# Ten of sixteen probability blocks turned by DMA instead of eight, with six slots for halves and eight for turned blocks, in a masked attention kernel on one core

## The reference

```
h      = maximum(layernorm(x), 0)                 # (8192, 128), eps 1e-5
scores = einsum('nd,md->nm', h, ks)               # (8192, 8192)
scores = leaky_relu(scores, negative_slope=0.2)
scores = where(adj > 0, scores, -9e15)
attn   = softmax(scores, axis=1)
out    = x + einsum('nm,md->nd', attn, ks)
```

## Time and profile before

| | |
|---|---|
| median of 3 runs | 1658.87 us (1658.17 to 1659.25) |
| the profiled execution | 1658.6 us |
| its span in the profile | 1656.8 us |
| busy: TensorE, VectorE, ScalarE, GpSimd | 97%, 90%, 85%, 70% |
| HBM read, written | 276.82 MB, 4.19 MB |

### The profile page before, as it was taken

The page is one execution under the profiler, slowest core; times in us unless marked ns, Lnnn a source line. Parts: engine busy times, 40 slices in busy tenths (PEclk is TensorE's granted clock), DMA queues, the critical chain, the costliest instruction groups (busy, mean ns, idle before and its releaser), DMA issues.

```text
span 1656.8 us, 38135 instructions
## 1 busy us (share of the span) xinstructions
PE 1609.1 (97%) x13442; PEld 1181.7 (71%) x13442; DVE 1491.6 (90%) x2592; ACT 1400.4 (85%) x2081; POOL 1155.8 (70%) x1224
## 2 busy tenths in 40 slices
PE   5699999999999999999999999999999999999999
PEld 3477777777777777777777777777777777777777
DVE  7999899899899899999999999999998998998996
ACT  6688888888888888888888888888888888888887
POOL 1576776776776767767767767767767767767766
PEclk8999999999999999999999999999999999999999
DMA  7799999999999999999999999999999999999996
GB/s 235 196 230 261 253 264 256 248 265 269 249 263 254 254 262 263 253 261 255 254 265 259 253 260 253 264 266 248 262 260 256 263 262 248 268 258 244 272 253 127
DMA packets 641340, 417.78 MB, mean 252 GB/s; under 512 B 551040, under 2 KB 575616, under 8 KB 641152
## 3 DMA queue, kind: packets, MB, share of 16 engines
q1 hardware_dynamic: 641152, 415.34, 103.9%
HBM read 276.82 MB, written 4.19 MB: 170 GB/s over the span
## 4 chain that ended last, share of the span: by engine, by line
PE 70%; DVE 18%; issue 4%; ACT 2%; POOL 1%; DMA 0%; DVEq 0%; POOLq 0%
PE ps_out L386 20%; PE ps_T L371 10%; PE ps_out L387 10%; PE ps_scores L360 10%; PE ps_scores L362 10%; PE ps_scores L361 10%; DVE mask L573 8%; DVE scores L591 5%; DVE probsT_lo L600 2%; ACT probsT_hi L470 2%; DVE hT_hi L516 1%; DVE row_min L606 1%; DVE plain_max L609 1%; POOL keys_in L314 0%; PE ps_out L338 0%
## 5 line engine op out<-in xcount | busy, mean ns | idle before, releaser
L314 POOL TENSOR_TENSOR keys_in<-scores,keys_in 128x512 f16<-128x512 f32 x512 | 652.2, 1274 | 41.4
L591 DVE CUSTOM_DVE_ANT_0 scores<-ps_scores,mask,minus_scale 128x1024 f32<-128x1024 f32 x512 | 652.8, 1275 | 1.4 <-PE ps_scores L362 0.6
L312 POOL CAST keys_in<-scores 128x512 f16<-128x512 f32 x512 | 346.0, 676 | 402.3 <-ACT scores L462 402.0
L462 ACT ACTIVATE scores<-scores,neg_max 128x1024 f32<-128x1024 f32 x512 | 582.5, 1138 | 0.0
L453 ACT ACTIVATE scores<-scores 128x1024 f32<-128x1024 f32 x512 | 537.8, 1050 | 51.9 <-DVE pair_min L591 51.8
L600 DVE TENSOR_TENSOR probsT_lo<-ps_T,probsT_hi 128x512 f16<-128x512 f32 x512 | 350.2, 684 | 130.1 <-ACT probsT_hi L470 130.1
L470 ACT ACTIVATE probsT_hi<-ps_T 128x512 f16<-128x512 f32 x512 | 305.7, 597 | 186.1 <-PE ps_T L371 185.7
L386 PE MATMUL ps_out<-keys,probsT_hi 128*128 128x256 f16 x2048 | 392.8, 272 | 18.8 <-DVE probsT_lo L600 12.8
L360 PE MATMUL ps_scores<-keysT_hi,hT_hi 128*128 128x512 f16 x1024 | 391.2, 382 | 16.4 <-DVE keysT_lo L555 9.4
L361 PE MATMUL ps_scores<-keysT_lo,hT_hi 128*128 128x512 f16 x1024 | 390.5, 381 | 0.0
L362 PE MATMUL ps_scores<-keysT_hi,hT_lo 128*128 128x512 f16 x1024 | 390.1, 381 | 0.0
(11 more groups left out here) (52 smaller groups left out, 830.0 us busy)
## 6 DMA issues: line engine op xcount, KB each, us to landing
adj_in<-in_adj_dram SPq DMA_DIRECT2D x512, 512.0 KB, 5.1
keys_in<-keys_in SPq DMA_TRANSPOSE x512, 4.9
x_in<-in_x_dram SPq DMA_DIRECT2D x64, 64.0 KB, 2.1
keys_in<-in_L_gnn_ks_dram SPq DMA_DIRECT2D x8, 512.0 KB, 7.3
out_dram<-out_tile SPq DMA_DIRECT2D x64, 64.0 KB, 1.8
```

The costliest lines, as they stand in the source:

```text
L314: nc.gpsimd.tensor_tensor(half[:, BLOCK:2 * BLOCK], probs(t, b), half[:, 0:BLOCK], ALU.subtract) \
L462: nc.scalar.activation(s, s, ACT.Exp, bias=neg_max[:, t % 2:t % 2 + 1], scale=-SLOPE, accum_out=pair_sum[:, t % 2, p:p + 1]).then_inc(prob ...
L591: nc.vector.tensor_tensor_reduce(out=score_pair(q, p), in0=ps_scores[:, slots, :].rearrange("p s k -> p (s k)"), in1=mask[:, (p // 2) % 2, ...
```

## The change

`BY_DMA` takes blocks 4 and 12 as well. It then holds ten blocks, 1, 3, 4, 5, 7, 9, 11, 12, 13, 15, and `BY_PE` six, 0, 2, 6, 8, 10, 14. The slots for halves go from four to six and those for turned blocks from six to eight, fourteen of the sixteen that there is room for. All counts and waits follow from these tuples and sizes.

```
-    R_SLOTS = 4
+    R_SLOTS = 6
     X_SLOTS = 4
-    D_SLOTS = 6
+    D_SLOTS = 8
...
-    BY_DMA = tuple(b for b in range(BLOCKS) if b % 2 == 1)
+    BY_DMA = tuple(b for b in range(BLOCKS) if b % 2 == 1 or b in (4, 12))
     BY_PE = tuple(b for b in range(BLOCKS) if b not in BY_DMA)
```

## The result

The change made the kernel slower: 1699.34 us in the median of 4 runs (1697.12 to 1710.2) against 1658.71 for the kernel before (4 runs, 1658.17 to 1659.25), a ratio of 1.0258 [1.0228, 1.0288]. The forecast was 1622 and its range ended at 1698. What happened is the outcome of rival (b), a step of 25.6 us and 1700.

The account below looks back on a forecast made before the run. TensorE bounds the kernel before at 25.02 us a step, DMA afterwards at 24.35. 62 steps save 41.5 us, tail and start add 3.6 + 1: span 1619.9, time 1622, 8 in 10 range 1588 to 1698.

Parts of the forecast that it names:

- rival (b): DMA saturates under the mixed traffic; at a share of 1.16 a step takes 25.6 us, total 1700; chance 0.30.
- the mixed stretch: Fullest window mixing loads and transposes before the change, share 1.22 for 10 us; gave DMA's need of 24.35 us a step.
- The rival's own point of decision: DMA share in mixed traffic: below 29.7 / 25.02 = 1.19, the step is longer than before.
- The floor by 210 GB/s: DMA step from separate rates: eight loads at 1.38 us, ten transposes at 1.25, some 0.4 for x and store: 23.9 us.
- TensorE's need: TensorE's step without two blocks' transposes (0.88 us) and two short waits (0.49 us): 23.65 us instead of 25.02.
- both waits: TensorE's waits each step, 0.14 us for hT_lo and 0.35 us for block 12's probsT_lo, expected to go.
- rival (a): DMA keeps up and GpSimd or TensorE bounds, 23.65 to 24.0 us a step, total 1589; chance 0.20.
- GpSimd's need: GpSimd's step: ten split_half 18.0 us, normalise 1.7, four mask meetings at 1.03 each: 23.8 us.
- collisions with masks: GpSimd waiting while VectorE makes a mask, four times a step at 1.03 us each.
- some 8: Microseconds until GpSimd has block 7's half ready after getting pair 2's probabilities: 7.1, some 8 with a mask.
- Rival (c): Hidden dependency chain around a step's end holds the step at 24.9 to 25.0 us, total 1656 to 1664; chance 0.08.
- the ring: Chain around a step's end: TensorE, probsT_hi, split_h, add_mask, minimum and a mask stretched to 2.1 us; step near 25.0 us.

Follow-up runs that it names:

- the new order alone: Kernel before (eight blocks by DMA) with split_h ahead of split_probs_lo in slot 14 and slot 0's mask made at slot 14's end: 1627.19 us, 0.9811.
- the turns apart: Kernel after, with SP issuing the adj load between a slot's two turns instead of ahead of both: 1739.43 us, 1.0487.
- the fastest kernel: Kernel after with nine blocks by DMA (4 not turned), split_h ahead of split_probs_lo and slot 0's mask at slot 14's end: 1608.65 us, 0.9702.

## Why the prediction was wrong

**The step that failed** is the choice of the ceiling, "I take 24.35: the mixed stretch is the row nearest to the new mixture". The work of DMA was right: predicted 29.7 us of packets a step, measured 1.15 x 25.67 = 29.5. The divisor was not. It was taken as 1.22, from ten microseconds; over whole steps the share is 1.13 to 1.15 in the kernels with nine to eleven blocks, while short windows go far above it, to 1.35 in the kernel after. 29.7 / 1.15 = 25.8 would have been slower than before. The other end of the range, 1.16, gave rival (b) its 25.6. That this lies so near is in part luck: the 1.16 came from a stretch of loads alone, without a transpose. No row of the kernel before shows the new mixture at its limit, so the trace could bound the ceiling poorly and not fix it. The rival's own point of decision, a share of 1.19, was the right question. And with 0.30 on a rival at 1700, a range of 8 in 10 that ends at 1698 was too narrow by the prediction's own numbers.

That it is the load on DMA, and not something that came with it, is shown: without the two transfers' bytes 1699 us become 1612, with half the bytes of `adj` and every issue in its place 1618; without the work on their halves nothing changes, and the slots change nothing. Not shown is which limit of DMA it is. The engines' packets may be at their ceiling, or too few transfers may fit in the queue at a time, or a turned block simply comes too late for a step of this order: fewer bytes relieve all three. A longer distance between turn and use (`ADD_LAG`) would tell the last from the others; it was not tried.

The Trainium skill ("DMA: Bandwidth & Descriptors", section "Latency and other measured facts") gives 261 GB/s for transposing DMAs with a non-contiguous middle dimension. The slices full of transposes in the earlier trace rows show 203 to 223 but for one stretch of 255 to 278, which "210 GB/s wherever a slice was full of them" passes over. So the figure agrees with that one stretch and not with the others. The floor by 210 GB/s, 23.9 us, was still 1.8 us short of the measured step: rates taken from loads alone and from turns alone don't give the mixture's.

**TensorE's need** was put at 23.65 us. With DMA out of the way it is 24.2 (24.20 and 24.21 with the extra turns or half of `adj` gone). TensorE is busy for 1475.89 / 1500 x 24.20 = 23.81 of it; the rest is the wait for `probsT_lo`, which moved from block 12's copy in slot 2 to block 8's in slot 14. The prediction had both waits go and looked for no new one. The upper value, 24.14 "if both waits stay", was nearer, though for another wait. So rival (a), 1589, was out of reach in this order of instructions: with DMA relieved the chip gives 1612.

**GpSimd's need** was put at 23.8 us and is 1276.96 / 1500 x 25.67 = 21.9 of busy time. That leaves 21.9 - 19.7 = 2.2 us for collisions with masks, where 4.1 had been counted. A sixth of its work taken away changed nothing.

**Latency.** The halves were as early as worked out, 8.2 us for "some 8". Landing grew little, 5.3 us for 4.9. The 4.4 us for which the finished half of block 7 stood behind other issues at SP were missing from the sum, as was the 6.0 us landing of this turn, for 4.9 in the median.

**Rival (c)** did not happen with ten blocks, and its 0.08 was fair: with DMA relieved, TensorE's wait for `add_mask` is not there. But the ring is near. With nine blocks it holds the step at 24.89. With eight, the new order alone takes the step from 25.02 to 24.50, which is 1.9% of the time: both short waits of TensorE that the prediction had read, 0.14 and 0.35 us, go with it. The prediction had looked for their end in the blocks that leave TensorE, and not in the order of VectorE's work.

**Tail and head.** The tail grew by 3.2 us where 3.6 had been added. The head became 1.0 us shorter where 1 us had been added.

**Still open** is why the same bytes cost so unlike amounts in another order, size or queue: 26.33 us with the turns apart, 27.97 with loads of 1 MB, 34.5 with the loads from ScalarE. The packets' time a step, share by step, is 29.5 in the kernel after but 1.15 x 26.33 = 30.3, 1.10 x 27.97 = 30.8 and 1.18 x 34.5 = 40.7 in these. So the time that the same bytes are under way isn't fixed but depends on their order, size and queue, and a share of 1.15 is what this program reached and no constant of the chip. TensorE's lower granted clock (0.98, 0.96 and 0.91 with loads of 1 MB from SP, from ScalarE, and 512 KB from ScalarE) may add to the three slowest; that wasn't separated. How packets of turns and of loads mix on an engine would be the thing to measure; it wasn't tried.

## What to carry to other kernels

Moving work from a full engine to DMA pays until the transfers hold each other up, and how much DMA can carry is not to be read from a share over ten microseconds: over whole steps it was 1.15 here, in single windows 1.35. Where no row shows the new mixture, the honest forecast is the range, and a run with one block moved can narrow it.

Add up the issue times of the engine that issues the transfers: 72% of its time before, 94% after. The median issue alone misleads: it was 1.23 us in the slower kernel with split loads and 1.73 in the fastest one. And 94% says that the transfers are at their limit, not that time is lost: the fastest kernel has it too.

Before a unit is relieved, look at whether it is its work or an order of instructions about a step's end that holds the step: here two moves in VectorE's order gave 1.9%, and with them one more turned block paid as well (3.0% together, where the block alone gave 0.3%).

## What the runs showed of the hardware

- Loads of 1 MB beside transposing DMAs were slower than loads of 512 KB, 248 GB/s against 271 over the middle, and so were loads of 256 KB, 266 GB/s. The Trainium skill ("DMA: Bandwidth & Descriptors", section "Rules for kernel authors") asks for at least 1 MiB per DMA for the most bandwidth. Beside these transposes no run agrees with it. These are the rates that this kernel drew, with its own waits in them, and not the most that DMA can give.
- Plain loads issued from ScalarE and transposes from SP, at the same time, took the rate down to 209 GB/s with loads of 512 KB, in a run in which TensorE's granted clock was 0.91; with loads of 1 MB the issuing engine made no difference (1847.97 and 1849.39 us).
- A transposing DMA of 256 KB takes SP 1.23 us at least to issue, also in the median with half the bytes of `adj` (1232 ns), and up to 3.9 us in the kernel after.
- The DMA share, which counts packets by time under way, is no measure of work: 1.18 was the share at 209 GB/s and 1.14 that at 275 (the fastest kernel).
- TensorE's granted clock stayed at 1.00 over the middle of the kernel after. With the loads from ScalarE it was 0.50 in 816 to 824 us, behind four microseconds without a matmul.
